# Keys, values and first queries of two cross-attention layers in one pipeline of token blocks

## The chip, the core and the metric

The kernel runs on one core of a Trainium2 chip. The metric is the device time of one execution in microseconds (us), and less is better. The core has a matrix engine (TensorE, PE in the rows; its weight loads are listed as PEld), a vector engine (VectorE, DVE), a scalar engine (ScalarE, ACT), GpSimd (POOL), and a queue that issues transfers (SyncE, SP). The engines run their own instruction streams and meet only at semaphores. TensorE runs at one of two clock levels, 1.2 and 2.4 GHz; the rows show the granted level as a fraction of the higher one (0.50 and 1.00).

## What is computed

Two cross-attention layers over 4096 query tokens (`x`) and 3202 context tokens (`ctx`), all 512 features wide:

```python
# layer 0: 8 heads of 16
Q0 = x @ W_q;  K0 = ctx @ W_k;  V0 = ctx @ W_v          # 512 -> 128 each
x1 = ffn(x + softmax(Q0 K0^T / 4) V0 @ W_o)
# layer 1: 16 heads of 32
kv = layernorm(ctx; mean, var) * gamma + beta
K1, V1 = split(kv @ Wkv.T)                               # 512 -> 512 each
Q1 = layernorm(x1) @ Wq.T
out = ffn(x1 + softmax(Q1 K1^T / sqrt(32)) V1 @ Wo + bo)
```

Only the products `Q0`, `K0`, `V0`, `K1`, `V1` and the norm of `ctx` are touched by the change. Everything after them is the same code in both kernels.

## The kernel before

All activations are kept feature-major: 512 features are four tiles of 128 partitions (`KT` = 4), and tokens run along the free axis in blocks of 512 (`NB`). Every float32 operand is split into a rounded part ("hi", float32r) made by ScalarE and a remainder ("lo") made by VectorE; each product is the three matmuls hi*hi, hi*lo, lo*hi. A product of 512 inputs is therefore 12 matmuls.

`build` (L1635) calls the phases one after the other. A phase (L43) ends by clearing its semaphores and a barrier of all engines. In order: `project("kv")` (L1653), `project("pq0")` (L1659), attention of layer 0 (`a0`), the middle (`m`: end of layer 0 and the queries of layer 1), attention of layer 1 (`a1`), the ending (`e`).

`project` (L115) does one input. First `split_weights` (L63) brings the weights through a two-deep stage, in pieces of one 128-row tile: SP loads, ScalarE copies to hi, VectorE subtracts to lo, and SP waits for that before it loads two pieces on. This block of code ends before the first token block is loaded. Then the token blocks run as a software pipeline: while the products of block n are made, the steps that prepare block n+1 are put in between by `interleave` (L208) at places given as fractions of the products. For the keys and values ("kv", 7 blocks, the last of 130 tokens) the steps of a block are: split x (L274, L327); mean by 8 matmuls with a matrix of 1/512 over both halves (L382); centre (L333); square and split the squares (L279, L281, L339); variance by 8 matmuls; square root (L286); reciprocal (L344); multiply by it (L345); gamma and beta (L348); split the normed block (L291, L354). Then 16 products of a block: 1 of K0, 4 of V0 (128 columns each), 4 of K1, 4 of V1 (the token tiles are the stationary side for the values), in a ring of 4 PSUM banks and 4 output buffers. The first product of a block waits for the last preparing step of it:

```python
if i == 0:
    pe.wait_ge(dve_steps, n * NDVE + NDVE)
pe.wait_ge(lo_done[s], before)
```

Keys are stored as [hi/lo, feature, token], values as [head, token in tile, tile, 16 or 32], so that a value store writes pieces of 64 or 128 bytes.

The queries ("pq0", 8 blocks) have one product a block, in one slot of the ring, so that ScalarE can only empty the next product when the 8 stores of the last one (64 KB each, one per head) have landed.

The middle phase (`m`, printed only in part here) already does a norm in another form for the queries of layer 1: `presum` (L1458, L1461) adds the four feature tiles on VectorE, one float32 matmul (L1583) gives the mean or variance, gamma is multiplied into the weights once (L1511), the product is made from the centred values, and its result is multiplied by 1/std (L1487) and gets the bias `beta @ W` (made once by single-column matmuls, L1605) on ScalarE and VectorE (L1384, L1491).

## Time and profile before

| | us |
|---|---|
| median of 3 runs (5737.87 to 5742.69) | 5738.86 |
| profiled execution, its own time | 5741.43 |
| its span | 5739.7 |
| weights of "kv" | 0 to 28.9 |
| "kv" until its first product | 28.9 to 68.3 |
| "kv" products | 68.3 to 306.6 |
| end of phase | 306.6 to 311.4 |
| "pq0" with its end | 311.4 to 392.1 |
| attention 0, middle, attention 1, ending | 392.1 to 5739.7 |

All times below are from the span's start of that execution. A busy time of TensorE counts overlapping records, so the distance between the starts of two matmuls says how fast they go, not the length of one record. "<-" names what an engine waited for.

### The profile page before, as it was taken

The page shows a single profiled execution, that of the slowest core. Times are in us where ns is not written, and L with a number is a line of the kernel's source. Part 1 is how long each engine was busy: PE and PEld are TensorE (multiplying, and loading weights), DVE is VectorE, ACT ScalarE, POOL GpSimd, SP SyncE. Part 2 cuts the span into 40 slices and gives each one's busy share as a digit, 9 for nine tenths or more (in the row PEclk, how much of TensorE's full clock was granted, in tenths as well). Part 3 has the DMA queues.
Part 4 walks back from the last instruction along what each step waited for, and adds up shares of the span by engine and source line. Part 5 has one row for each costly group of instructions (what it writes and reads, how often), then busy time and mean ns, then how long its engine had stood idle before and what let it go on. Part 6 is the DMA issues. An engine that isn't in the chain of part 4 may idle for free. (4 is left out here: it accounts for less than half of the span.)

```text
span 5739.7 us, 103849 instructions
## 1 busy us (share of the span) xinstructions
PE 5364.3 (93%) x28676; PEld 3368.1 (59%) x28676; DVE 3997.0 (70%) x6906; ACT 3200.2 (56%) x5849; POOL 2329.3 (41%) x1156
## 2 busy tenths in 40 slices
PE   5959999999979799999999999999999998899999
PEld 4834444444447565655565656555565664677777
DVE  4439888888847688888787878878788886332231
ACT  3317777777733256666666666666666665222222
POOL 0000000000000068888787888878788887000000
PEclk9969999999979899999999999999999999899999
DMA  3451111111144321111111111111111111322220
GB/s 99 125 132 30 37 37 37 37 36 37 28 140 120 108 66 41 39 41 28 40 39 42 39 29 39 41 39 40 28 39 41 41 28 44 111 96 81 81 88 22
DMA packets 328588, 325.61 MB, mean 57 GB/s; under 512 B 184624, under 2 KB 192688, under 8 KB 326064
## 3 DMA queue, kind: packets, MB, share of 16 engines
q1 hardware_dynamic: 328112, 319.92, 21.0%
q8 instruction: 218, 3.57, 0.3%
q14 instruction: 258, 2.11, 0.1%
HBM read 219.18 MB, written 100.53 MB: 56 GB/s over the span
## 5 line engine op out<-in xcount | busy, mean ns | idle before, releaser
L777 DVE TENSOR_REDUCE a_maxes<-a_mscore 128x1 f32<-128x458 f32 (+4 forms) x5376 | 3039.4, 625 | 668.7 <-PE a_mscore L836 640.3
L760 ACT ACTIVATE a_prob<-a_score 128x512 f32<-128x512 f32 x4992 | 2633.6, 598 | 1271.2 <-PE a_score L845 1260.6
L845 PE MATMUL a_score<-a_q,a_k 97*128 97x512 f32 (+1 forms) x4992 | 1993.4, 434 | 54.3 <-DMA a_q<-row 31.6
L836 PE MATMUL a_mscore<-a_k,a_qm 96*128 96x458 f32 (+4 forms) x5376 | 1901.1, 417 | 69.8 <-DMA a_k<-k 56.0
L864 PE MATMUL a_acc<-a_prob,a_v 128*32 128x512 f32 x9984 | 1613.0, 608 | 0.0
L836 PEld LDWEIGHTS a_mscore<-a_k,a_qm 96*128 96x128 f32 (+1 forms) x5376 | 1479.1, 310 | 192.1 <-issue 71.9
L726 POOL TENSOR_TENSOR a_added<-a_added,a_prob 128x1024 f32<-128x1024 f32 x640 | 1527.8, 2387 | 55.5 <-POOL a_added L726 0.2
L845 PEld LDWEIGHTS a_score<-a_q,a_k 97*128 97x128 f32 (+1 forms) x4992 | 924.8, 195 | 1028.1 <-ACT a_prob L760 534.9
L723 POOL TENSOR_TENSOR a_added<-a_prob 128x1024 f32<-128x1024 f32 x128 | 305.3, 2385 | 2053.7 <-ACT a_prob L760 2043.3
L859 PE MATMUL a_acc<-a_prob,a_ones 128*1 128x512 f32 x2048 | 965.1, 593 | 0.0
L864 PEld LDWEIGHTS a_acc<-a_prob,a_v 128*32 128x32 f32 x9984 | 293.4, 109 | 304.4 <-issue 155.7
L1136 DVE TENSOR_TENSOR e_hl<-e_h,e_hh 128x512 fp32r<-128x512 f32 x128 | 88.5, 692 | 457.4 <-ACT e_hh L1085 457.4
L1081 ACT ACTIVATE e_h<-e_hp,e_bias 128x512 f32<-128x512 f32 x128 | 88.2, 689 | 548.5 <-PE e_hp L1193 548.5
L739 POOL TENSOR_TENSOR a_total<-a_total,a_vsum 128x512 f32<-128x512 f32 x128 | 165.9, 1296 | 387.0 <-DVE a_vsum L791 386.9
L859 PEld LDWEIGHTS a_acc<-a_prob,a_ones 128*1 128x1 f32 x2048 | 129.0, 82 | 310.9 <-issue 310.9
L791 DVE TENSOR_REDUCE a_vsum<-a_prob 128x128 f32<-128x384 f32 x512 | 288.7, 585 | 22.3 <-ACT a_prob L760 22.3
L1193 PE MATMUL e_hp<-e_xh,w_hi 128*128 128x512 f32 x512 | 203.3, 397 | 4.1 <-DVE e_xl L1128 4.1
L1193 PE MATMUL e_hp<-e_xh,w_lo 128*128 128x512 f32 x512 | 203.1, 397 | 0.0
L1193 PE MATMUL e_hp<-e_xl,w_hi 128*128 128x512 f32 x512 | 203.0, 397 | 0.0
L736 POOL TENSOR_TENSOR a_total<-a_added 128x512 f32<-128x512 f32 x128 | 166.3, 1299 | 19.4 <-POOL a_added L730 18.1
L730 POOL TENSOR_TENSOR a_added<-a_added,a_prob 2x512 f32<-2x512 f32 x128 | 163.9, 1281 | 11.2 <-ACT a_prob L760 0.2
L746 ACT ACTIVATE a_acc_sb<-a_acc 97x512 f32<-97x512 f32 (+1 forms) x192 | 114.9, 598 | 72.2 <-PE a_acc L859 60.4
(188 smaller groups left out, 3905.9 us busy)
## 6 DMA issues: line engine op xcount, KB each, us to landing
a_qm<-q SPq DMA_DIRECT2D x384, 64.0 KB, 1.8
a_q<-q SPq DMA_DIRECT2D x384, 64.0 KB, 1.8
acc<-a_acc_sb SPq DMA_DIRECT2D x384, 64.0 KB
e_part<-acc SPq DMA_DIRECT2D x90, 256.0 KB, 3.4
a_k<-k SPq DMA_DIRECT2D x48, 416.0 KB, 5.8
q<-m_qout SPq DMA_DIRECT2D x128, 128.0 KB, 2.3
e_wo<-wo_split SPq DMA_DIRECT2D x32, 512.0 KB, 4.1
k<-kv_out SPq DMA_DIRECT2D x30, 512.0 KB, 2.7
```

What stands on the lines that cost most here:

```text
L723: pool.tensor_tensor(added[:], prob[:, 1:3], prob[:, 4:6], ALU.add).then_inc(add_done, 1)
L726: pool.tensor_tensor(added[:], added[:], prob[:, 3 * i + 1:3 * i + 3], ALU.add).then_inc(add_done, 1)
L736: pool.tensor_tensor(total[:], added[:, 0], added[:, 1], ALU.add).then_inc(add_done, 1)
L739: pool.tensor_tensor(total[:], total[:], vsum[:], ALU.add).then_inc(add_done, 1)
L760: act.activation(prob[:, t], score[SCORES[it.j][t]][:], ACT.Exp, scale=SCALE).then_inc(exp_done, 1)
L777: dve.tensor_reduce(maxes[j][:, t, c:c + 1], mscore[u % UNIT_BANKS][:, 0:wide], AX.X, ALU.max).then_inc(unit_read, 1)
L791: dve.tensor_reduce(vsum[:, cols], prob[:, ON_VECTOR[0]:ON_VECTOR[-1] + 1, cols].rearrange("p t c -> p c t"), AX.X, ALU.add).then_inc(vsum ...
L836: pe.matmul(mscore[u % UNIT_BANKS][:, 0:wide], qm[j][r:r + ROW, t:NB:NB // P], kt[kk][r:r + ROW, at:at + wide], start=True, stop=True).the ...
L845: pe.matmul(score[SCORES[it.j][t]][:], kt[it.k][r:r + C, i * P:(i + 1) * P], qt[it.j][r:r + C, :], start=True, stop=True).then_inc(score_d ...
L859: mm = pe.matmul(acc[c * 32:c * 32 + 1, :], ones[:], total[:] if what[0] == "sum" else prob[:, what[1]], start=(i == 0), stop=not after)
L864: mm = pe.matmul(acc[c * 32:c * 32 + 32, :], vt[kk][:, L.FIRST[half] + at, :], prob[:, what], start=(i == 0), stop=not after)
L1193: mm = pe.matmul(hp[m % 2][:], W1[a][:, k, m * P:(m + 1) * P], (xh, xl)[c][:, k], start=(t == 0), stop=(t == 3 * KT - 1))
```

## The change

`project` and `split_weights` go. One phase, `front`, does all of it, unrolled in full. Weights come as five whole transfers, between those of the tokens. The eight query blocks stand at the head; the first K0/V0 products, the weights' gains and the bias products lie between them. The norm takes the form that the middle has: VectorE adds feature tiles (`presum`), one float32 matmul gives the mean or variance, the products of K1 and V1 are made from the centred block, and the division comes behind them. For keys 1/std is a row vector (`rstd`, after `var`); for values it is a column per token tile (`rstdc`, after `varc`, four single-column matmuls). K0 and V0 of block n+2 are made in the middle of block n. The last block is 130 tokens wide, without padding; the pad columns are stored as zeros from an own transfer. Helpers that are cut only issue one instruction with its waits.

```diff
-    project(nc, "kv", ctx_t, S,
-            {"k0": a["L0_xattn_W_k"], "v0": a["L0_xattn_W_v"], "k1": a["L1_xattn_Wkv"][:, 0:D], "v1": a["L1_xattn_Wkv"][:, D:2 * D]},
...
-    project(nc, "pq0", x, T, {"q0": a["L0_xattn_W_q"]}, [("raw", "q0", "items", q[0])])
+    front(nc, "kv", ctx_t, x, a["L0_xattn_W_k"], a["L0_xattn_W_v"], a["L1_xattn_Wkv"], a["L1_xattn_ln_kv_g"],
+          a["L1_xattn_ln_kv_b"], a["L0_xattn_W_q"], k, v, q[0])
...
+        prod = [ps(f"prod{i}", [P, NB]) for i in range(5)]
+        mean, var, varc = ps("mean", [P, NB]), ps("var", [P, NB]), ps("varc", [P, KT])
...
+        @block.sync
...
+            load_weight("wq", small[0], w_q0)
+            load_xq(0)
+            load_xq(1)
+            load_weight("wk0", small[1], w_k0)
+            load_weight("wv0", small[2], w_v0)
+            load_ct(0)
...
+            load_weight("wk1", yc[:], w_kv1[:, 0:D])
+            load_xq(2)
+            load_weight("wv1", sq[:], w_kv1[:, D:2 * D])
+            load_xq(3)
+            load_ct(1)
...
+            for i in range(QBLOCKS):
+                if i + 4 < QBLOCKS:
+                    load_xq(i + 4)
+                store_q(i)
+                if i == 1:
+                    store_first(0)
+            load_ct(2)
+            store_first(1)
+            for n in range(BLOCKS):
+                for m in range(KT):
+                    store_keys(n, m)
+                if n + 3 < BLOCKS:
+                    load_ct(n + 3)
+                if n + 2 < BLOCKS:
+                    store_first(n + 2)
+                for m in range(VT[n]):
+                    store_values(n, m)
...
+        @block.scalar
...
+            halve_q(2)
+            split_xq(4)
+            act.wait_ge(bias_made, 2)
+            act.activation(biask[:], var[:, 0:KT], ACT.Copy).then_inc(bias_done, 1)
+            act.activation(biasv[:], mean[:], ACT.Copy).then_inc(bias_done, 1)
+            halve_q(3)
+            split_xq(5)
+            act.wait_ge(bias_done, 2)
+            square(0)
+            halve_q(4)
+            split_xq(6)
+            split_x(1)
+            halve_q(5)
+            split_xq(7)
+            deviation(0)
...
+        @block.vector
...
+            def presum(src, to, w, i, before, done):
+
+                dve.tensor_tensor(pair[:, :, 0:w], src[:, 0:2, 0:w], src[:, 2:4, 0:w], ALU.add).then_inc(pair_done, 1)
+                dve.wait_ge(pair_done, i + 1)
+                dve.wait_ge(*before)
+                dve.tensor_tensor(to[:, 0:w], pair[:, 0, 0:w], pair[:, 1, 0:w], ALU.add).then_inc(done, 1)
...
+            split_weight(4, WV1, gained[1])
+            sum_x(0)
+            halve_q(3)
+            split_xq(5)
+            centre(0)
+            halve_q(4)
+            split_xq(6)
+            sum_squares(0)
+            split_x(1)
+            halve_q(5)
+            split_xq(7)
+            invert(0)
+            halve_q(6)
+            split_yc(0)
+            halve_q(7)
+            halve_first(1)
+            for n in range(BLOCKS):
+                if n + 1 < BLOCKS:
+                    sum_x(n + 1)
+                if n + 2 < BLOCKS:
+                    split_x(n + 2)
+                scale_key(n, 0)
+                scale_key(n, 1)
+                if n + 1 < BLOCKS:
+                    centre(n + 1)
+                halve_key(n, 0)
+                halve_key(n, 1)
+                scale_key(n, 2)
+                if n + 1 < BLOCKS:
+                    sum_squares(n + 1)
+                scale_key(n, 3)
+                halve_key(n, 2)
+                if n + 1 < BLOCKS:
+                    split_yc(n + 1)
+                halve_key(n, 3)
+                if n + 2 < BLOCKS:
+                    halve_first(n + 2)
+                if n + 1 < BLOCKS:
+                    invert(n + 1)
+                for m in range(VT[n]):
+                    value(n, m)
...
+        @block.tensor
...
+            def find_variance(n):
+                pe.wait_ge(sqsum_done, n + 1)
...
+                for m in range(VT[n]):
+                    tokens = min(P, W[n] - m * P)
+                    pe.matmul(varc[0:tokens, m:m + 1], sqsum[:, m * P:m * P + tokens], inv_d[:, 0:1], start=True,
+                              stop=True)
+                pe.matmul(var[:, 0:W[n]], inv_d[:], sqsum[:, 0:W[n]], start=True, stop=True).then_inc(var_done, 1)
...
+            def key(n, m):
+                if m == 0:
+                    pe.wait_ge(ycl_done, n + 1)
+                    pe.wait_ge(w_lo, len(W_ORDER))
+
+                    if n + 1 < BLOCKS:
+                        pe.wait_ge(v0_done, n + 2)
...
+                elif n == 0:
+                    pe.wait_ge(ql_done, QBLOCKS)
+                else:
+                    pe.wait_ge(v1_done, (n - 1) * KT + m)
+                products(prod[m], WK1, slice(m * P, (m + 1) * P), (ych[n % 2], ycl[n % 2]), W[n]).then_inc(k1_made, 1)
...
+            queries(0)
+            queries(1)
+            first(0)
+            queries(2)
+            biases()
+            queries(3)
+            find_mean(0)
+            queries(4)
+            queries(5)
+            find_variance(0)
+            queries(6)
+            queries(7)
+            first(1)
+            for n in range(BLOCKS):
+                key(n, 0)
+                key(n, 1)
+                if n + 1 < BLOCKS:
+                    find_mean(n + 1)
+                key(n, 2)
+                key(n, 3)
+                if n + 2 < BLOCKS:
+                    first(n + 2)
+                if n + 1 < BLOCKS:
+                    find_variance(n + 1)
+                for m in range(VT[n]):
+                    value(n, m)
```

`biases` is 16 single-column float32 matmuls (`beta @ W` for keys, into `var`) and 4 of 512 columns (for values, into `mean`). `first(n)` is the 12 matmuls of K0 and the 48 narrow ones of V0. The value step `value(n, m)` on VectorE reads PSUM once: product times `rstdc` plus `biasv`.

## Rows read from the trace of the kernel before

**Rows 1.** The page's first part: busy time, share, instructions of each engine

```profile
PE 5364.3 (93%) x28676; PEld 3368.1 (59%) x28676; DVE 3997.0 (70%) x6906; ACT 3200.2 (56%) x5849; POOL 2329.3 (41%) x1156
```

**Rows 2.** Busy time of each engine by stage, up to the attention

```profile
core 0: us, PE busy (x) PEld busy (x) DVE busy (x) ACT busy (x) POOL busy (x), PEclk, DMA share, GB/s
0.00:28.90 28.90, 0.00 (x0) 0.00 (x0) 7.88 (x16) 8.79 (x17) 0.20 (x4) 1.00 0.29 91
28.90:68.30 39.40, 7.36 (x16) 4.96 (x16) 17.27 (x14) 11.41 (x7) 0.00 (x0) 0.88 0.24 80
68.30:306.60 238.30, 226.69 (x1140) 191.63 (x1140) 112.12 (x99) 82.12 (x116) 0.00 (x0) 0.96 0.48 121
306.60:311.40 4.80, 0.00 (x0) 0.00 (x0) 0.00 (x0) 0.58 (x1) 0.00 (x0) 0.98 0.47 74
311.40:392.10 80.70, 34.94 (x96) 25.18 (x96) 24.59 (x20) 21.21 (x20) 0.00 (x0) 0.69 0.61 160
```

**Rows 3.** Waits from 28.9 to 312: us in total, times, longest us

```profile
PE kv_prod L408 <- DVE kv_zl L354: 23.5, 6, 12.8
```

**Rows 4.** Waits from 312 to 392, the same columns

```profile
PEld pq_prod L408 <- DVE pq_xl L327: 39.2, 6, 21.2
ACT pq_out L302 <- DMA q<-pq_out: 17.6, 7, 7.5
```

**Rows 5.** VectorE in order of time, two blocks' centring: start, us, operation

```profile
114.08 2.29 DVE L333 TENSOR_TENSOR kv_xc<-kv_xt,kv_mean 128x2048 f32<-128x2048 f32 x1 [1.80 <-PE kv_mean L382]
...
151.77 2.29 DVE L333 TENSOR_TENSOR kv_xc<-kv_xt,kv_mean 128x2048 f32<-128x2048 f32 x1 [1.79 <-PE kv_mean L382]
```

**Rows 6.** TensorE in order of time, in "kv" and in the middle phase

```profile
90.27 0.39 PE L408 MATMUL kv_prod<-kv_zh,kv_k_hi 128*128 128x512 f32 x1
...
95.96 0.39 PE L408 MATMUL kv_prod<-kv_v_hi,kv_zl 128*128 128x512 f32 x1
...
111.30 0.28 PE L408 MATMUL kv_prod<-kv_v_hi,kv_xh 128*128 128x128 f32 x1
111.41 0.28 PE L408 MATMUL kv_prod<-kv_v_hi,kv_xl 128*128 128x128 f32 x1
...
1636.68 4.71 PE L1605 MATMUL m_var<-m_gb,m_sq 128*128 128x1 f32 x32
...
1756.17 1.02 PE L1583 MATMUL m_mean<-m_ysum,m_inv_d 128*128 128x512 f32 x2
1757.26 0.40 PE L1555 MATMUL m_prod<-m_xl,m_w_hi 128*128 128x512 f32 x1
```

**Rows 7.** Stretches: start of the products, around a block's start, a load of queries

```profile
68.30:72.30 4.00, 3.95 (x9) 3.17 (x10) 2.11 (x1) 0.00 (x0) 0.00 (x0) 0.50 0.00 0
...
104.00:106.00 2.00, 0.06 (x1) 0.00 (x0) 2.00 (x1) 1.82 (x2) 0.00 (x0) 1.00 0.92 145
106.00:108.00 2.00, 1.76 (x5) 1.39 (x6) 1.50 (x2) 0.57 (x1) 0.00 (x0) 0.60 0.92 144
...
321.00:323.00 2.00, 0.00 (x0) 0.00 (x0) 0.00 (x0) 0.00 (x0) 0.00 (x0) 0.50 1.05 402
```

**Rows 8.** Groups of VectorE: form, count, busy us and mean ns of one, idle before

```profile
L327 DVE TENSOR_TENSOR kv_xl<-kv_xt,kv_xh 128x2048 fp32r<-128x2048 f32 x6 | 13.7, 2292 | 9.7 <-ACT kv_xh L274 9.7
L363 DVE TENSOR_TENSOR kv_out<-kv_prod,kv_out 128x512 fp32r<-128x512 f32 x30 | 20.7, 689 | 62.2 <-ACT kv_out L302 62.2
L344 DVE RECIPROCAL kv_rstd<-kv_std 128x512 f32<-128x512 f32 x6 | 20.1, 3353 | 10.7 <-ACT kv_std L286 10.7
L1491 DVE SCALAR_TENSOR_TENSOR m_qout<-m_scaled,m_biasq,m_qout 128x512 fp32r<-128x512 f32 x32 | 23.8, 745 | 1.1
```

**Rows 9.** The middle phase, one block's stretch, columns as in rows 2

```profile
1757.00:1798.00 41.00, 38.76 (x162) 29.98 (x160) 30.18 (x35) 15.36 (x20) 0.00 (x0) 1.00 0.45 135
```

**Rows 10.** Transfers from 312 to 392: count, size, median us from issue to landing

```profile
pq_xt<-in_x SPq DMA_DIRECT2D x8, 1024.0 KB, 5.6
```

**Rows 11.** Start of the attention in order of time

```profile
392.15 1.28 ACT L760 ACT_TABLE_LOAD   x1 [6.91 <-PEq L60]
```

More of the change, by code:

```diff
@@ L905, in _ @@
                             weigh(it.n, it.k, b)
-def blocks_of(eng):
-    B = T // NB
-    with eng.Fori(0, B // 2 - 1) as i:
-        yield i * 2, 0, i, True, True
-        yield i * 2 + 1, 1, i, True, True
-    yield B - 2, 0, B // 2 - 1, True, False
-    yield B - 1, 1, B // 2 - 1, False, False
 TERMS = ((0, 0), (0, 1), (1, 0))
```

671 lines of the change are left out of this document (388 added, 283 removed).

## The prediction

> **What bounds the kernel now.** The page's first line comes first: TensorE is busy for 93% of the span [rows 1], so on the average it is the bound, but an average says nothing about the part that is changed. The second view is the busy time by stage [rows 2]. The change replaces what lies before 392.1; the rest of the span, 5739.7 - 392.1 = 5347.6, is the same code. In those 392.1 TensorE is idle for the 28.9 of the weights, nearly idle for the next 39.4 (7.4 busy), close to full in the 238.3 of the products, idle for 4.8 at the phase's end, and less than half busy in the 80.7 of the queries. So the first 68.3 are a start-up that nothing covers, the middle 238.3 are TensorE's, and the queries are bound by something else.
>
> The waits say by what. In the products of keys and values the one wait of TensorE that counts is for the last step of the norm, the low half of the normed block: 23.5 in six times, of which 12.8 once at the start, so about 2.1 a block later [rows 3]. In the queries the weight load waits for the split of x (39.2), and ScalarE waits for the eight stores of the last product before it may empty the next one (17.6) [rows 4]: a chain of load, split, product, store, with one slot.
>
> A period of "kv" is 151.77 - 114.08 = 37.7 [rows 5]. It can be counted. From 90.27 to 95.96 stand 25 steps of 512-column matmuls, 0.2275 each; a 128-column one follows the last at 0.11 [rows 6]. A block has 12 + 48 + 48 of the wide (24.6), 48 narrow (5.3), and 16 wide for mean and variance (3.7): 33.6. With the 2.1 of waiting that is 35.7. The missing 2.0 is clock: after the idle time at the block's start the granted clock reads 0.60 in a stretch of 2.0, where it was 1.00 before, and at the first product 9 matmuls took 4.0 at 0.50, which is 0.44 each [rows 7]. So 2.1 idle costs about 4 in all.
>
> **The change, part by part: the loop.** The new loop has per full block 24.6 of wide products and 5.3 of narrow ones as before. Mean and variance are now one float32 matmul each. The middle has them: two records from 1756.17, and the products behind go on at their own pace from 1757.26 [rows 6]; less one 0.23, that is 0.86 for the two records of one matmul, 1.7 for both in place of 3.7. New are the four single-column matmuls for `varc`; the middle's 32 records of this kind took 4.71, 0.147 each [rows 6], and four are eight records, 1.2. Sum 32.8.
>
> Does anything else need longer? VectorE, from the rows of its forms [rows 8], per block: three passes of 2048 (split x, centre, split the centred) 6.9; two partial sums, each half a 2048 pass and a 512 one, about 3.7; eight 512-wide passes on keys (4 x 0.69 + 4 x 0.745) 5.7; four for values at 0.745, 3.0; K0's remainder 0.7; reciprocal 3.4. Sum 23.4, 9 below TensorE. ScalarE was busy 82.1 of the 238.3 of the products [rows 2], 13 a block, and loses one pass of 2048: about 11. VectorE's order matters more than its sum: from the start of key(n, 0) the block's own chain is centre(n+1) once the mean is made at 6.4 (ends 8.9), square 10.9, sum of squares 12.9, split 16.6, while `find_variance` stands at 20 in TensorE's stream and key(n+1, 0), which needs the split, at 32.8. The reciprocal ends at about 26 and delays value(n, 0), made at 24; its bank is needed again at 35.5. So I find no wait in the steady state and cost the waits at 0.5 a block, with 0 and 4.8 (the old period back) as ends. The middle's steady stage is the nearest case: TensorE busy 38.8 of 41.0 at clock 1.00 [rows 9].
>
> The removed `rstd` product, gamma and beta passes and the split of the squares (two passes of 2048, four of 512, and one of 2048 on ScalarE) lay beside TensorE's work; their removal pays only by ending the 2.1 wait and the clock that it costs.
>
> Blocks 0 to 3: 4 x 32.8 = 131. Block 4 makes the short first(6), 28.9. Block 5 has no `first` and short statistics, 22.9. Block 6 has 48 matmuls of 130 columns and 24 of 512, 11. Waits 3. The loop is 197.
>
> **The head.** It is a chain over three engines. VectorE's work in it: 8 splits of query blocks 18.3, their 8 remainders 5.5, three small weights 2.1, eight gain products of 512 at 0.69 or less 5.5, two large weight remainders 4.6, two splits of context 4.6, betas 1.2, sum of x 1.9, centre 2.3, squares 1.9, reciprocal 3.4, split 2.3, two K0 remainders 1.4: 55. TensorE's at the high level: queries 21.8, two `first` 16.0, biases 4.7/2 x 2 = 4.7 (16 single-column matmuls are 32 records) plus 4 x 0.86, together 8.1, statistics 2.9: 49. Transfers: 8 MB of queries, 2 of context, 2.75 of weights in, about 5 out, at 402 GB/s [rows 7] 44; a single MB needs 5.6 [rows 10]. I therefore walk the order of the three streams. Estimated times from the span's start: first query block in at 6.5, split 10.7; products 0 and 1 done 18.2 (the first at 0.44 a matmul); context block 0 split 17.3, first(0) 18 to 26; query 2, 29; biases 29 to 37; query 3, 39.7. Meanwhile VectorE has made gains, splits and weight remainders without a gap and sums x by 38.9. Mean 40.6; but VectorE takes halve_q(3) and split_xq(5), both behind the bias copies on ScalarE, before centre(0), which ends at 47.9. Square 49.8; halve_q(4) and split_xq(6) come before the sum of squares, which ends at 56.5. TensorE has been idle since about 50. Then variance at the low level 3.5, query 6 and 7 7, first(1) 8, and ScalarE's copy of V0, for which key(0, 0) waits: 76. On VectorE's side the split of the centred block ends near 70. Block 2's context is queued behind all query stores (eight issues each) and lands at about 80; it is needed by TensorE at 88.
>
> So loop start 76, with 66 (VectorE's 55, a first load, and the last V0) and 108 (next part) as ends.
>
> **The end.** After the last product: one VectorE pass, a store of 256 KB, semaphores, barrier. "kv" has the same end today, 4.8 from the last TensorE work to the next phase [rows 2]. The barrier between the two phases and the second ramp fall away; they are inside the 392.1. The attention would start at 76 + 197 + 5 = 278 in place of 392.1 [rows 2, 11]: 114 less. Its own start (memsets, then loads) sees the same state, so nothing is given back later. The profiled execution would take 5741.4 - 114 = 5627. It lies 2.6 above the median of the runs, so the median comes to 5738.9 - 114 = 5625.
>
> Where the 114 comes from: the queries' stage 81 shrinks to what the head needs beyond today's start-up (76 - 68 = 8), 73; the products 238 to 197, 41.
>
> **A rule against it.** Seven blocks now cycle TensorE through eight banks, with a semaphore at every group of 12 matmuls. The rows show that a 2.1 gap was followed by a clock of 0.60 [rows 7], and that the middle, built alike, keeps 1.00 with 2.2 idle in 41.0, spread over several groups [rows 9]. The Trainium skill, "TensorE: Matmul & The Clock Gate", section "A second HAM failure mode: psum-queue depth-cycling", says that small idle times between groups as banks are cycled can make the clock swing between its two levels. By the page the loop could run long stretches at 1.2 GHz; by the middle's row it does not, and I side with the row and keep the other as a rival.
>
> **The rivals.**
> 1. *The head is TensorE's at the low level.* The queries' stage today reads a clock of 0.69 [rows 2], because its bursts are short. If the head's gaps do the same throughout, its 49 become 97 behind the first split at 10.7: loop start 108, time 5625 + 32 = 5657. For it: VectorE's 55 leaves gaps between products. Against it: first(0), biases and query 3 stand in one row, 21 of work without a wait.
> 2. *The loop keeps the old period.* A wait takes the removed one's place: SP stores keys, block load, K0/V0 and values in strict order, and the value stores in small pieces run at 145 GB/s with the transfer engines 0.92 busy [rows 7]. Six periods of 37.6: +29, 5654. Against it: 4.75 MB a block, of which 1.25 are slow, need 8.6 + 3.5/0.402 = 17 of 33.
> 3. *The clock falls in the loop* (the rule above): each wait between groups throws TensorE back to 0.44 a matmul. The whole loop would take nearly 197 more; the kernel becomes slower once more than 114 of the loop's 197 at the high level, 58%, run at the low one. Nine tenths of it: 5625 + 177 = 5802, slower than before.
> 4. *The change doesn't do what it says*: the head's three streams block each other so often that the queries still take their 81 beside the start-up of 68, and the loop keeps its period: 149 + 226 + 5 = 380, or 5739 - 12 = 5727.
>
> **How the numbers follow.** Forecast 0.70 (5625; its own ends are 5612, with head 66 and no waits, and 5645, with head 90 and waits of 1.5 a block). Rival 1 0.12, rival 2 0.13, rival 3 0.03, rival 4 0.02. The range 5605 to 5662 takes in the forecast and rivals 1 and 2, with 5 to 7 at either end for what the walk through the head may miss. A measurement of this kernel can tell about 0.2%, 11, from no change. Faster by more than that: 0.95; same 0.02; slower 0.03.
>
> **What would show it.** In the trace of the changed kernel: the first attention row near 278; VectorE's centring at a period of 32.8 to 33.5; TensorE's clock 1.00 from the first key product on; granted clock in the head between 0.6 and 0.9; the mean matmul at 0.86 and a `varc` record at 0.15; in the head, centre(0) about 7 after the mean is made, and TensorE idle before the variance of block 0; no wait of TensorE for VectorE over 1 in the loop. Wrong would be: waits for stores in the loop, a period over 35, key(0, 0) later than 90, or an attention, middle or ending that differs from 5347.6 by more than 5.

## The result, and the profile after

The changed kernel takes 5599.95 us, the median of 4 runs (5594.11 to 5608.29), against 5738.98 for the kernel before (5737.87 to 5742.69): a ratio of 0.9758, 95% interval 0.9741 to 0.9775. That is 139 faster where 114 were forecast, and 5 below the low end of the range. The profiled execution took 5599.11, with a span of 5597.3.

The page's first line of the changed kernel, which answers to [rows 1]:

```profile
PE 5326.1 (95%) x28684; PEld 3349.3 (60%) x28684; DVE 4013.6 (72%) x6947; ACT 3170.5 (57%) x5792; POOL 2330.6 (42%) x1156
```

Busy time by stage of the new phase, columns as in [rows 2]: the head until its chain breaks, the wait for the norm of block 0, the last of the head, the loop, the end:

```profile
0.00:57.00 57.00, 38.12 (x174) 29.56 (x174) 37.25 (x39) 30.27 (x27) 0.20 (x4) 0.93 0.96 303
57.00:67.00 10.00, 8.32 (x23) 6.28 (x24) 9.92 (x7) 3.65 (x4) 0.00 (x0) 0.54 0.40 70
67.00:78.57 11.57, 10.79 (x74) 9.71 (x72) 6.10 (x6) 4.20 (x5) 0.00 (x0) 1.00 0.65 109
78.57:268.70 190.13, 190.13 (x986) 159.13 (x987) 123.74 (x137) 56.77 (x68) 0.00 (x0) 1.00 0.61 147
268.70:275.90 7.20, 1.64 (x8) 0.41 (x5) 0.74 (x1) 0.00 (x0) 0.00 (x0) 0.90 0.48 73
```

In the loop TensorE is busy for all of its 190.13 at a granted clock of 1.00, where the products of before had 226.69 of 238.30 at 0.96 [rows 2]. All waits of TensorE from 0 to 270 (us in total, times, longest) stand in the head:

```profile
PE kv_prod L1043 <- DVE kv_ycl L866: 11.7, 1, 11.7
PE kv_varc L1110 <- DVE kv_sqsum L895: 7.3, 1, 7.3
PE kv_mean L1101 <- DVE kv_xsum L895: 1.5, 1, 1.5
PE kv_prod L1043 <- ACT kv_v0out L767: 0.8, 1, 0.8
```

The first is the start (no query block is split before 11.7), the second the wait ahead of the variance of block 0. The third and fourth are small. The granted clock of the head falls twice. The second fall stands behind the 7.3. The first comes with TensorE busy without a gap since 11.7, about 2 into the 32 single-column records of the key bias:

```profile
29.96 4.89 PE L1087 MATMUL kv_var<-kv_gb,kv_yc 128*128 128x1 f32 x32
```

```profile
30.00:32.00 2.00, 2.00 (x21) 2.00 (x19) 2.00 (x2) 0.28 (x1) 0.00 (x0) 1.00 1.00 330
32.00:34.00 2.00, 2.00 (x12) 2.00 (x11) 0.63 (x1) 0.00 (x0) 0.00 (x0) 0.52 1.07 368
34.00:36.00 2.00, 2.00 (x6) 1.48 (x7) 0.00 (x0) 0.10 (x1) 0.00 (x0) 0.50 0.97 287
```

The 0.93 of the first stage is even somewhat too high: the clock reads 1.00 there from 0 on, but the first products, from 11.67, go at 0.43 a matmul, which is the pace of the low level. The three engines in order of time (start, us, operation): the first key product; a mean, the second matmul of the product around it and VectorE's centring in two blocks; the single-column matmuls with the variance behind them; ScalarE's copy of V0 in two blocks; and the attention's first row:

```profile
78.57 0.47 PE L1043 MATMUL kv_prod<-kv_ych,kv_wk_hi 128*128 128x512 f32 x1 [0.78 <-ACT kv_v0out L767]
...
116.63 1.02 PE L1101 MATMUL kv_mean<-kv_xsum,kv_inv_d 128*128 128x512 f32 x2
...
117.69 2.29 DVE L917 TENSOR_TENSOR kv_yc<-kv_ct,kv_mean 128x2048 f32<-128x2048 f32 x1 [0.17 <-PE kv_mean L1101]
...
117.72 0.39 PE L1043 MATMUL kv_prod<-kv_ycl,kv_wk_hi 128*128 128x512 f32 x1
...
131.00 1.00 PE L1110 MATMUL kv_varc<-kv_inv_d,kv_sqsum 128*128 128x1 f32 x8
...
131.20 0.60 ACT L767 ACTIVATE kv_v0out<-kv_prod 128x512 f32<-128x512 f32 x1 [4.71 <-PE kv_prod L1050]
...
131.86 1.10 PE L1112 MATMUL kv_var<-kv_sqsum,kv_inv_d 128*128 128x512 f32 x2
...
150.21 2.29 DVE L917 TENSOR_TENSOR kv_yc<-kv_ct,kv_mean 128x2048 f32<-128x2048 f32 x1 [0.17 <-PE kv_mean L1101]
...
163.72 0.60 ACT L767 ACTIVATE kv_v0out<-kv_prod 128x512 f32<-128x512 f32 x1 [4.71 <-PE kv_prod L1050]
...
275.93 1.28 ACT L411 ACT_TABLE_LOAD   x1 [10.37 <-PEq L60]
```

A period is 163.72 - 131.20 = 32.52, and so is the centring's, 150.21 - 117.69, against 37.7 in [rows 5]. The attention starts at 275.93 in place of 392.15 [rows 11]: 116.2 earlier. That is what the changed code brings, and 142.4 (5739.7 - 5597.3) is what the span lost. The other 26 lie in stages whose code is the same. Each stage is read from one profiled execution of each kernel. Here are those stages of the kernel before: attention 0 from its first row to its last row maximum, its end (to the middle's first product), the middle, attention 1, the ending:

```profile
392.15:1560.25 1168.10, 1119.54 (x6660) 554.12 (x6660) 1029.97 (x1870) 887.10 (x1688) 0.00 (x0) 0.96 0.18 37
1560.25:1632.30 72.05, 34.40 (x127) 8.79 (x124) 13.12 (x16) 25.25 (x45) 0.00 (x0) 0.55 0.38 113
1632.30:1988.95 356.65, 322.45 (x1312) 248.11 (x1312) 245.24 (x265) 127.24 (x164) 0.00 (x0) 0.96 0.40 119
1988.95:4920.61 2931.66, 2819.50 (x15921) 1692.08 (x15921) 2316.63 (x4265) 1828.16 (x3468) 2329.14 (x1152) 0.98 0.16 41
4920.61:5739.66 819.05, 799.45 (x3408) 643.23 (x3408) 230.23 (x344) 208.29 (x327) 0.00 (x0) 0.99 0.23 76
```

And the same stages of the changed kernel:

```profile
275.93:1439.60 1163.67, 1115.95 (x6659) 553.17 (x6660) 1030.15 (x1869) 887.28 (x1688) 0.00 (x0) 0.96 0.18 37
1439.60:1500.60 61.00, 23.39 (x127) 6.75 (x125) 13.19 (x17) 24.64 (x45) 0.00 (x0) 0.74 0.43 134
1500.60:1859.14 358.54, 324.15 (x1312) 249.06 (x1312) 245.21 (x265) 127.69 (x164) 0.00 (x0) 0.96 0.40 119
1859.14:4781.65 2922.51, 2815.03 (x15921) 1691.38 (x15921) 2317.17 (x4265) 1828.27 (x3467) 2330.37 (x1152) 0.98 0.16 41
4781.65:5597.33 815.68, 798.54 (x3408) 643.79 (x3408) 230.10 (x344) 207.73 (x327) 0.00 (x0) 0.99 0.24 77
```

The counts are the same, the times are not: -4.4, -11.1, +1.9, -9.2, -3.4, together -26.1. Two of them have a place that can be seen.

**The end of attention 0**: 72.05 with a clock of 0.55, or 61.00 with 0.74. Low time, worked out as length x (1 - clock) x 2, is 65 against 32. It begins at the last row maximum. The first 24.0 behind it, before and after:

```profile
1560.21:1584.21 24.00, 22.74 (x91) 6.15 (x90) 3.61 (x3) 15.77 (x30) 0.00 (x0) 0.65 0.03 7
...
1439.66:1463.66 24.00, 22.35 (x125) 6.62 (x125) 3.61 (x3) 20.76 (x40) 0.00 (x0) 1.00 0.03 7
```

After, ScalarE has made its 40 exponentials by then; before, TensorE fell to its low level on the way, and only 30 of them are done.

**Attention 1**: it works through 128 items, each one head and one block of 512 queries; they are counted here from one row maximum to the next. In five of them (33, 49, 65, 81 and 97) the loop over pairs of heads jumps back. These five together take 144.4 before and 127.2 after, 17.2 less, while the rest of the stage is 8.1 longer after. Item 81 takes 29.61 against 25.04. These are the waits inside it; "issue" is time in which the engine waited for nothing that the profile shows. Before:

```profile
ACT a_prob L760 <- PE a_score L845: 14.8, 9, 3.8
...
PE a_mscore L836 <- issue: 2.6, 1, 2.6
...
PE a_score L845 <- issue: 2.0, 1, 2.0
```

After:

```profile
ACT a_prob L411 <- PE a_score L496: 10.1, 9, 3.6
...
PE a_score L496 <- issue: 2.0, 1, 2.0
```

The stop of 2.6 in front of a `mscore` is gone, and the granted clock over the item is 0.93 in place of 0.88. It is so in all five: before, TensorE stops 2.2 to 2.6 in front of a `mscore`, 12.5 together, and after it never does. The low time of the five is 34 before and 17 after.

### The profile page after: what moved, and what is told of

The parts are those of the page before. It is cut to its first block and busy times, and to the rows that moved or that the text cites. A ratio compares the mean times of both kernels' runs of the same rounds, so it can differ in the third digit from the quotient of the medians.

```text
span 5597.3 us, 103454 instructions
## 1 busy us (share of the span) xinstructions
PE 5326.1 (95%) x28684; PEld 3349.3 (60%) x28684; DVE 4013.6 (72%) x6947; ACT 3170.5 (57%) x5792; POOL 2330.6 (42%) x1156
## 5 line engine op out<-in xcount | busy, mean ns | idle before, releaser
L387 POOL TENSOR_TENSOR a_total<-a_added 128x512 f32<-128x512 f32 x128 | 165.9, 1296 | 21.1 <-POOL a_added L381 19.8
L397 ACT ACTIVATE a_acc_sb<-a_acc 97x512 f32<-97x512 f32 (+1 forms) x192 | 114.8, 598 | 65.1 <-PE a_acc L510 57.0
```

The lines of the kernel that those rows point to most:

```text
L387: pool.tensor_tensor(total[:], added[:, 0], added[:, 1], ALU.add).then_inc(add_done, 1)
```

## The experiments

Two questions: is the gain of the front what it was forecast to be, for the reasons given; and what moves 26 us in code that nobody touched? For the second there were three candidates: the time since the start (or the transfers that are still under way), the phase of the clock, and the place of the code. In what follows "front" is the time to the attention's first row, "end" the end of attention 0 with its low time in brackets, "five" the sum of the five items, each from one profiled execution. The two references: before 392.1, 72.1 (65), 144.4; after 275.9, 60.9 (32), 127.2.

### A pause at the start of attention 0

VectorE writes an unused tile 8 times (e1) or 210 times (e2) ahead of its fills; e3 is the changed kernel once more, and e4 is the kernel before with the pause of e1.

```diff
+        PAUSE = 8 if name == "a0" else 0
...
+            for i in range(PAUSE):
+                dve.wait_ge(paused, i)
+                dve.memset(pad[:], 0.0).then_inc(paused, 1)
             for ap, value in FILLS:
                 dve.memset(ap, value).then_inc(filled, 1)
```

> The changed kernel with about 5 us of vector memsets (8 of 512 columns) ahead of attention 0's own; nothing else is changed. In the profiles of before and after, attention 0 (its activation table load to the middle's first product) took 1240.2 and 1224.7 with the same instructions; of the 15.5, 11 lie behind the last row maximum, where the granted clock is 0.50 for the last items of before and 1.00 for those of after. Theory P (the clock's falls land by the moment at which the attention starts and ends): attention 0 takes some value between 1224 and 1241 that need not be the changed kernel's; the total is 5 longer than the changed kernel's, plus or minus 15. Theory S (the new front leaves something that makes the attention faster: buffers, code, transfers): attention 0 stays at 1224.7 within 2, total 5 longer.

> The changed kernel with about 116 us of vector memsets (210) ahead of attention 0's, so that the attention starts near the 392 of the kernel before. Theory P: attention 0 takes a value between 1224 and 1241; if the moment counted from the kernel's start decides, it is before's 1240 and the total is that of the kernel before less 0 to 10. Theory S: attention 0 at 1224.7 within 2, total 116 above the changed kernel, 23 under the kernel before.

> The changed kernel as it is, to see how much one kernel's stages move from run to run. Theory P: with the moments unchanged up to the jitter of the transfers, attention 0 and 1 may each move by up to 10; total 5594 to 5610. Theory S: 1224.7 and 2922.5 again within 2.

> The kernel before with the same 5 us pause ahead of attention 0. Theory P: attention 0 between 1224 and 1241, total 5744 plus 5, less up to 25: it can get faster through a pause. Theory S: 1240.2 within 2, total 5744.

| | median (lowest to highest) | ratio, 95% | front | end | five |
|---|---|---|---|---|---|
| e1 | 5606.25 (5595.27 to 5615.08) | 0.9746, 0.9728 to 0.9764 | 275.5 | 72.0 (65) | 122.4 |
| e2 | 5736.65 (5728.3 to 5753.05) | 0.9981, 0.9969 to 0.9993 | 276.0 | 72.3 (65) | 125.2 |
| e3 | 5599.64 (5595.45 to 5606.44) | 0.9743, 0.9725 to 0.976 | 274.8 | 61.4 (34) | 128.5 |
| e4 | 5747.7 (5740.65 to 5760.72) | 1.0001, 0.9991 to 1.001 | 390.4 | 62.1 (35) | 145.9 |

The first 24.0 behind the last row maximum in e1, and in e4:

```profile
1444.32:1468.32 24.00, 22.74 (x91) 6.14 (x90) 3.61 (x3) 15.77 (x30) 0.00 (x0) 0.65 0.03 7
...
1563.45:1587.45 24.00, 22.35 (x125) 6.62 (x125) 3.61 (x3) 20.76 (x40) 0.00 (x0) 1.00 0.03 7
```

In these profiles about 5 us of pause (5.1 by the rate of e2) turn the end of the changed kernel into that of the kernel before, to the last exponential, and the other way round in e4. So the end has two values and belongs to neither kernel.

The medians do not carry these 11. e1 is 6.6 above e3 and e4 is 3.0 above the 5744.75 of the kernel before in the same comparison, so less the pause of 5.1 they differ by +1.5 and -2.1, not by +11 and -10. The profiled executions of e1 and e2 are the slowest and the second slowest of theirs. The executions of one kernel lie up to 25 apart, and the slower ones show a lower mean clock (e1: 0.975 at 5595.27, 0.970 at 5615.08). The likely reading is that the end takes either value from one execution to the next; it isn't shown, as only one execution of each has a profile.

The pause of e2 was longer than meant:

```profile
L450 DVE MEMSET a_pad<- 128x512 f32 x210 | 101.8, 485 | 41.2 <-DVE a_pad L450 36.2 <-PEq L60 5.0
```

101.8 + 36.2 = 138.0. With that taken off, its median is 5598.7, that of the changed kernel: time since the start explains none of the 26. The five items take 122 and 125 in e1 and e2, 128.5 in e3, and 146 in e4. Whatever makes them long goes with the program of the kernel before, not with a moment that is 5 later. And the stop in front of `mscore` is there in all five items of e4 (2.4 to 2.6), and in none of e1, e2 and e3.

### TensorE's gaps at the end of attention 0 filled

In the last item of attention 0 a further matmul of 256 columns follows each score product (26 in all; the result is not read), in the kernel before (e5) and in e1 (e6).

```diff
                     scores(it, t)
+                    if it.last and name == "a0":
+                        if t == 0:
+                            pe.wait_ge(unit_read, H * QB * UNITS)
+                        for u in range(1):
+                            pe.matmul(mscore[u % UNIT_BANKS][:, 0:256], qm[it.j][0:ROW, 0:P], kt[it.k][0:ROW, 0:256],
+                                      start=True, stop=True)
                     due(it, t)
```

> The kernel before, with one matmul of 256 columns more behind each of the 26 score products of attention 0's last item; nobody reads their results. They are pure extra work for TensorE, about 0.12 each at the high level, 3 in all. Theory P (in the last item ScalarE is the bound and TensorE has gaps; whether its clock falls there, to 0.50, is decided by the moment, and at 0.50 TensorE becomes the bound): filled gaps keep the level at 1.00, the time from the last row maximum to the middle's first product goes from 72.1 to 60 to 64, in spite of the extra work. Rival (the low clock goes with the end, but doesn't set its length; the stage is longer for another reason, such as the stores): 72 to 75, and the whole no faster.

> The changed kernel with the 5 us pause, whose end of attention 0 took 72.0 with 65 of low clock, and the same 26 extra matmuls. Theory P: 60 to 64, and the whole about 10 faster than with the pause alone. Rival: 72 to 75.

| | median | ratio, 95% | front | end | five |
|---|---|---|---|---|---|
| e5 | 5722.46 | 0.9964, 0.9951 to 0.9976 | 391.1 | 65.7 (41) | 123.7 |
| e6 | 5607.32 | 0.9764, 0.9745 to 0.9783 | 276.8 | 65.1 (40) | 123.0 |

The first 24.0 of the end in e5:

```profile
1563.54:1587.54 24.00, 22.50 (x126) 8.76 (x124) 3.60 (x3) 17.89 (x35) 0.00 (x0) 0.86 0.03 7
```

The clock falls later (0.86 over the 24.0), and the end lands between its two values: 24 and 25 less low time, 6.4 and 6.9 less end. Expected was a clock that stays up, and an end of 60 to 64. Both kernels come out alike, so the low time is tied to the end's length, but the fill has not removed it. For e6 the whole was also expected about 10 faster than e1, and it is not (5607.32 against 5606.25). The fill also brought a surprise: the five items of the kernel before fell from 144 to 124, though nothing in attention 1 was edited. What it changed for that stage is where TensorE's later instructions lie, and the whole became 19.8 faster.

### TensorE's program moved by a few instructions

20, 7 or 30 unused single-column matmuls ahead of the first work of TensorE. Each is two records, and they go at 0.213 a record, the pace of the low level: 20 take 8.7, 7 take 3.2 and 30 take 13.0. In the kernel before, TensorE has no other work until 39.6, so 7 and 20 end in its idle time, while 30 put off its first statistic from 39.61 to 42.63. Their result is not read. Kernel before (e7: 20, e13: 7, e14: 30):

```diff
             if ln is not None:
                 pe.wait_ge(consts_done, 3)
+                for _ in range(20):
+                    pe.matmul(prod[0][:, 0:1], inv_d[:], inv_d[:, 0:1], start=True, stop=True)
```

Changed kernel (e8: 20, e15: 30):

```diff
+            pe.wait_ge(consts_done, 2)
+            for _ in range(20):
+                pe.matmul(varc[:, 0:1], inv_d[:], inv_d[:, 0:1], start=True, stop=True)
             queries(0)
```

> The kernel before with 20 single-column matmuls ahead of its first statistic, while TensorE waits for the first block; they only shift the place of all later TensorE instructions in its program. In attention 1 the five items at which the loop over pairs of heads jumps back (33, 49, 65, 81, 97) took 144.4 in the kernel before and 145.8 with the pause, against 127.2, 122.5 and 128.6 in the three profiles of the changed one. Theory L (where the code lies decides how long the engines wait for instructions after the jump): this sum moves by more than 5, either way, the rest stays. Rival (it is set by what ran before, or by chance): 144 to 146 again.

> The changed kernel with the same 20 matmuls at its start. Theory L: the sum over the five items leaves 122 to 129 by more than 5, either way, if the shift crosses a boundary; it can also stay. Rival: 122 to 129. The front itself: its start waits for the first queries anyway, so attention 0 starts at 275 to 277 as before, unless TensorE's level at the first product differs.

> The kernel before with 7 single-column matmuls ahead of its first statistic, in TensorE's idle time. With 20 of them the five items with a jump in attention 1 took 127.3 in place of 144.4, and the median fell by 31. Theory L (place of the code): the sum over the five items is near 144 or near 125, by where the shift of 7 puts the loop; all else of attention 1 within 8. Rival (20 extra matmuls changed something else, such as the moment): a value between, 130 to 140.

> The same with 30. Theory L: near 144 or near 125 again. Rival: between. If both shifts give 125, the kernel before stood at an unlucky place, and the median is near 5712 to 5725; where the end of attention 0 also stays at the high clock it is 5712, otherwise 5723.

> The changed kernel with 30 of them at its start. Theory L: its place is a good one, a shift can at best leave it: five items 119 to 129, or near 144, with a median of 5600 or 5617. Attention 0 starts at 275 to 278 either way.

| | median | ratio, 95% | front | end | five |
|---|---|---|---|---|---|
| e7, before, 20 | 5711.54 | 0.9948, 0.9933 to 0.9963 | 392.9 | 61.1 (32) | 127.3 |
| e13, before, 7 | 5719.06 | 0.9957, 0.9943 to 0.9972 | 394.5 | 61.1 (34) | 132.8 |
| e14, before, 30 | 5717.48 | 0.9955, 0.994 to 0.997 | 395.1 | 72.8 (66) | 129.8 |
| e8, after, 20 | 5599.22 | 0.975, 0.9733 to 0.9766 | 275.8 | 61.5 (32) | 123.4 |
| e15, after, 30 | 5609.37 | 0.9765, 0.9748 to 0.9781 | 278.1 | 73.0 (66) | 128.8 |

Item 81 in e7, waits as above:

```profile
ACT a_prob L762 <- PE a_score L847: 10.7, 9, 4.2
...
PE a_score L847 <- issue: 2.4, 1, 2.4
```

It reads like the changed kernel's item: the 2.6 ahead of `mscore` is gone. Each of the three shifts makes the kernel before 24 to 31 us faster by the medians, although the front gets 0.8 to 2.9 longer by work that is of no use; the shifts of 20 and 30 do not make the changed kernel faster. A later moment alone did not do this in e4. So the kernel before stood at a bad place, and leaving it is worth about the 25 that the forecast missed. In which stages the 24 to 31 lie can't be read from one profile each: the profiled executions lie 8 (e7), 8 (e13) and 18 (e14) above their medians, and e14's, the slowest of five, has the long end.

The expectation for e13 set 144 or 125 for the place of the code against 130 to 140 for something else, and 132.8 lies in the second range. The traces settle it. The stop in front of `mscore` stands in all five items of before and e4 and in no item of the five in the 15 other profiles, e13 among them. What is left is clock. The low time of the five is 34 in both profiles with the stop, and 0 (e12) to 27 (e13) in the others, whose sums are 119.1 plus half of it, to within 1.5 (e10: 3.1). For before that line gives 136; the 8 above it, of 17.2 between the two references, is what can be put down to the stops, and the other half is low clock. The rest of attention 1, expected to stay, is 5 to 8 longer in e7, e13 and e14 than the 2787 of before, and 9 longer in e4.

Held against the shifted kernels, the change is worth what was forecast: the three ratios of before average 0.9953, those of e3, e8, e15 and the changed kernel 0.9754, and (0.9953 - 0.9754) x 5739 = 114. The interval of each ratio is about 9 us to either side, so that it is 114 to the us is luck.

### The terms of the front

**e9: VectorE's passes put back.** Two unused passes of 2048 (2.28 each) in each of the first five blocks of the loop, one before `sum_squares`, one behind `split_yc`.

```diff
+            def again(i):
+                dve.wait_ge(junk_done, i)
+                dve.wait_ge(yc_done, i // 2 + 2)
+                dve.tensor_tensor(junk[:], yc[:], yc[:], ALU.subtract).then_inc(junk_done, 1)
...
+                if n + 1 < B:
+                    again(2 * n)
                 if n + 1 < BLOCKS:
                     sum_squares(n + 1)
...
                     split_yc(n + 1)
+                if n + 1 < B:
+                    again(2 * n + 1)
```

> The changed kernel with two more VectorE passes of 2048 elements in each of the loop's first five blocks (23 us in all), one ahead of the sum of squares and one behind the split of the centred block: where the old form of the norm had the split of the squares and the multiplication by 1/std. Their results are not used. Theory T (the loop is TensorE's, VectorE has 9 a block to spare, and the removed passes were worth nothing by their own length): attention 0 starts at 275 to 278, as in the changed kernel. Rival V (the shorter chain on VectorE is what pays): 2.3 to 4.6 a block, attention 0 at 287 to 299.

Median 5604.9, ratio 0.9753 (0.9736 to 0.9769); front 276.7, 0.8 later. That VectorE loses work is worth nothing by itself. Of the 5.2 that a period lost (37.7 to 32.5), 1.1 is TensorE's own work for the statistics (3.7 to 1.7 + 0.86), and the other 4 are the wait and its clock, counted at about 4 from the rows of before. That these went because no step of VectorE stands last before a product is argued from the order of the streams, and no run has put them back.

**e12: the statistics twice.** Mean and variance matmuls of blocks 1 to 6 issued twice, TensorE's work alone being longer.

```diff
+                if n > 0:
+                    pe.matmul(mean[:, 0:W[n]], inv_d[:], xsum[:, 0:W[n]], start=True, stop=True)
                 pe.matmul(mean[:, 0:W[n]], inv_d[:], xsum[:, 0:W[n]], start=True, stop=True).then_inc(mean_done, 1)
...
+                if n > 0:
+                    pe.matmul(var[:, 0:W[n]], inv_d[:], sqsum[:, 0:W[n]], start=True, stop=True)
                 pe.matmul(var[:, 0:W[n]], inv_d[:], sqsum[:, 0:W[n]], start=True, stop=True).then_inc(var_done, 1)
```

> The changed kernel with the float32 matmul of the mean and that of the variance issued twice in every block but the first: 10 of 512 columns and 2 of 130 more. Theory T (the loop is TensorE's, each record on its path): 10 x 0.86 + 2 x 0.3 = 9 later, attention 0 at 284 to 286. Rival (the loop is bound by VectorE, ScalarE or stores, and TensorE waits anyway): 0 to 3.

Median 5611.39, ratio 0.9767 (0.975 to 0.9784); front 286.7, 10.8 later. Each us of TensorE counts in full, and TensorE waits for nothing in the loop: the loop is bound by it. Of the 1.8 above the 9, most is one fall of the clock behind the single-column matmuls (0.70 and 0.50 in the two stretches of 2 from 134), which e11 shows more plainly.

**e10: the queries in their own phase again**, behind the new pipeline, by the old `project`.

```diff
-            queries(0)
-            queries(1)
             first(0)
-            queries(2)
             biases()
...
+    project(nc, "pq0", x, T, {"q0": a["L0_xattn_W_q"]}, [("raw", "q0", "items", q[0])])
```

> One half of the change alone: the new pipeline for keys and values, but without queries in its head; they are made behind it by the old phase. Theory (the walk through the head): without the queries' 24 on VectorE and 22 on TensorE the first key product comes at about 45 in place of 78.6; loop 192 and end 5 give 242, and the old query phase 81: attention 0 at 323, so 69 of the 116 come from the keys' and values' pipeline and 47 from the queries' place. Rival (the head is set by the weights' and the norm's chain, the queries only fill its gaps): first key product at 65 or later, attention 0 at 343 or more, and the queries' place is worth 67 or more.

Median 5664.77, ratio 0.9858 (0.9837 to 0.9878). The variance of block 0, the first key product, and SP's first transfer for the queries:

```profile
43.74 1.87 PE L1415 MATMUL kv_varc<-kv_inv_d,kv_sqsum 128*128 128x1 f32 x8 [6.36 <-DVE kv_sqsum L1216]
...
57.91 0.47 PE L1348 MATMUL kv_prod<-kv_ych,kv_wk_hi 128*128 128x512 f32 x1 [0.78 <-ACT kv_v0out L1106]
...
255.29 0.83 SPq L589 DMA_DIRECT2D pq_stage<-in_L_xattn_W_q  x2
```

The front is 335.4. So the 116.2 split in two: 392.1 - 335.4 = 56.7 for the new form of keys and values, and 335.4 - 275.9 = 59.5 for the queries' place (they take 80.1 apart, and 78.57 - 57.91 = 20.7 in the head). Expected were 69 and 47, and by the rival 67 or more for the queries; neither came. The first key product was expected at 45 and came at 57.91. From the start of the mean to that of the variance the norm's chain (mean, centre, square, sum) takes 43.74 - 36.29 = 7.5 here, and TensorE waits for 6.4 of it, having no query to make. In the changed kernel the same stretch is 58.68 - 44.74 = 13.9, as VectorE has two splits and a remainder of queries within it.

**e11: the centring of block 0 earlier.** In VectorE's order `centre(0)` and `sum_squares(0)` each go ahead of a query's remainder and split.

```diff
             sum_x(0)
+            centre(0)
             halve_q(3)
             split_xq(5)
-            centre(0)
+            sum_squares(0)
             halve_q(4)
             split_xq(6)
-            sum_squares(0)
```

> The changed kernel with another order on VectorE in the head: centre(0) straight behind sum_x(0), and the sum of squares ahead of halve_q(4) and split_xq(6). Theory (the 7.3 that TensorE idles before the variance of block 0, and the low clock behind it, come from VectorE's order): the variance starts at 53 in place of 58.7, the first key product and attention 0 come 4 to 6 earlier, at 270 to 272. Rival (something else is as late, such as ScalarE's square behind its query work): 0 to 2.

Median 5601.16, ratio 0.9743 (0.9726 to 0.9759): no gain. The wait before the variance is gone, but TensorE waits 2.4 and 5.0 for splits of queries and 3.0 for the mean's sum instead (1.5 after), and the first key product comes at 78.08, only 0.5 earlier. From mean to variance it is now 54.62 - 45.46 = 9.2. So VectorE's order does make that wait, as the theory had it, but the time is not to be had: the wait moves. In the profiled execution, the slowest of the four (5611.17 against 5597.78 for the fastest), the attention even started 6.2 later, at 282.1, and the cause is not in the head. Four stretches of its loop, the single-column matmuls standing from 97.99 to 98.85:

```profile
97.00:99.00 2.00, 2.00 (x20) 2.00 (x20) 1.15 (x2) 0.60 (x1) 0.00 (x0) 1.00 0.28 103
99.00:101.00 2.00, 2.00 (x4) 0.88 (x5) 0.00 (x0) 0.23 (x2) 0.00 (x0) 0.51 1.03 251
101.00:103.00 2.00, 2.00 (x7) 1.64 (x6) 1.53 (x2) 0.61 (x2) 0.00 (x0) 0.64 0.98 266
103.00:105.00 2.00, 2.00 (x10) 1.61 (x9) 2.00 (x2) 0.03 (x1) 0.00 (x0) 1.00 0.93 335
```

The granted clock falls for about 3.5 right behind them, with TensorE busy without a gap, and again at 133, 167 and 201, behind the same matmuls of the next three blocks. Four times 3.5 at half speed cost 7. The changed kernel's TensorE has the same instructions in the same order in its loop and keeps 1.00 in its profile. What decides between the two isn't known.

## Why the prediction was right in the front and wrong in the sum

**The head: right within 3.** First key product at 78.57, forecast 76. The idle time stands where the walk through the three streams put it: TensorE waits 7.3 before the variance of block 0 (6.5 forecast), which starts at 58.68 (56.5). Part of this is luck: the mean came 4.1 late (44.74 for 40.6), and the centring made up for half of it, as only one step of a query was left before it. The clock was low for the first products, for 6.8 from 32.1, and for 10.2 around that wait; the second of the three, behind the biases' single-column records, was not in the walk. Rival 1, the low level throughout, would have given 108. The cause of the wait was named rightly: without the queries on VectorE the chain takes 7.5 (e10), with three steps of them within it 13.9, and with another order the wait is gone (e11). But it is not time lost to that order, since e11 gains only 0.5.

**The loop: right.** Forecast 32.8 and 0.5 of waiting a block, measured 32.5 and none. The mean matmul took 0.86 (116.63 to 117.72, the second matmul of the product behind it, less one 0.23 for the first), as counted from [rows 6]. The eight `varc` records took 0.86 (131.00 to 131.86), 0.108 each, where 0.147 from [rows 6] was used: a term 0.3 too large. That row was a mean over both levels of the clock. In the kernel before, the level falls within those 32 records, without a wait of TensorE, and the records stand 0.112 apart before 1639 and 0.213 behind it:

```profile
1636.68:1638.68 2.00, 2.00 (x20) 2.00 (x18) 1.76 (x3) 1.94 (x4) 0.00 (x0) 1.00 0.54 136
1638.68:1641.39 2.71, 2.71 (x15) 2.62 (x14) 2.25 (x2) 0.42 (x1) 0.00 (x0) 0.56 0.41 81
```

Rival 2 (the old period) is refuted by the period, and by e9, where 4.6 more of VectorE per block changes nothing.

**The clock rule: small, and real in a form that was not foreseen.** The Trainium skill, "TensorE: Matmul & The Clock Gate", section "A second HAM failure mode: psum-queue depth-cycling", speaks of small idle times between groups. In the loop there is no idle time, the clock is 1.00 throughout in the changed kernel, and rival 3 did not come; so no run here tests the page's case. What does come is a fall at the single-column matmuls without any idle time: in the loop four times in e11 and once in e12, at about 1.75 each, and in the head of the changed kernel once, for 6.8.

**The end: right.** The last product starts at 269.95, one step of 0.23 later the loop is over, and the attention starts 5.7 behind that, for 5. The sum of the front is 78.6 + 191.6 + 5.7 = 275.9 where 76 + 197 + 5 = 278 was forecast; of the 5 that the loop is shorter, 3 are the waits that did not come.

**The failed step** is "its own start sees the same state, so nothing is given back later", with the sentence before it that the rest of the span, 5347.6, is the same code. Same code was taken for same time. The rest took 5321.4. What the runs show in its place is that the time of this code depends on where TensorE's program lies: with nothing but 7, 20 or 30 unused matmuls ahead of it, the kernel before is 24 to 31 faster by the medians, and it is not faster with a pause that moves the moment alone (e4). In the two profiled executions the 26.1 lie as follows. 11.1 are the end of attention 0, which has two values: e1 and e4 show that each kernel's program can have either, and the medians don't bear them out as a lasting difference between the kernels. 17.2 are the five items in attention 1, of which 8.1 come back elsewhere in that stage. That the stop in front of `mscore` goes with the place of TensorE's code is shown by e5, e7, e13 and e14, where nothing of that stage was changed, and by both profiles that have the program of the kernel before unmoved (144 and 146, with the stop) against all the 15 others (119 to 133, without it); the low clock in these items makes up the other half. The last 5.9 (-4.4, +1.9, -3.4) have no cause that was found. The prediction had named a difference of over 5 there as a sign of being wrong, but gave the range no room for it: the terms outside the change carried no bounds at all. With 26 as their size, its low end would have been 5612 - 26 = 5586.

**Still open.** Which address or boundary matters for the stop; 7, 20 and 30 matmuls all leave the bad place. What sets how often the clock falls in the five items (low time 0 to 27 without the stop). How the 24 to 31 of the medians divide over the stages. Why the stage from the attention's first row to its last row maximum varies between 1162 and 1173 from kernel to kernel (pauses taken off). And that the end of attention 0 is chosen by the clock's phase is argued from the low time (32 to 35, or 65 to 66, with nothing between unless the gaps are filled); what sets the phase, and whether it changes from one execution to the next, was not measured.

No version beat the changed kernel: e3 and e8, at 5599.6 and 5599.2, are the same within their intervals.

## What to carry to other kernels

Where a norm stands before a product on the bound engine, move its division behind the product and add the feature tiles on the idle engine first: the gain can be counted as matmul steps at the rows' own spacing, to within 3 in 116 here. A small phase bound by a chain of load, split, product and store is worth more inside the start-up of a large one (20.7 in place of 80.1). And give the untouched rest of a long kernel bounds of its own: here it moved by 26 between two profiles, and 7 to 30 unused matmuls ahead of it moved the whole by 24 to 31, so a change of this size is only judged against a kernel before that has been shifted too.

## What the hardware showed that was not expected

- Code that is the same, instruction for instruction, takes 61 or 72 at the end of a phase, by whether TensorE falls to its low level in the last item (low time 32 or 65). In one profile each, a pause of 5 turned it both ways; in the medians it left no such difference.
- Unused matmuls at the start of the program, 7, 20 or 30 of them, made the kernel before 24 to 31 faster. A stop of 2.2 to 2.6 in each of five items at a loop's jump, for which the profile names no cause, went away with them.
- A gapless stream of matmuls can lose its clock at single-column records: within 32 of them in the head of the changed kernel (from 32.1, for 6.8) and in the middle of the kernel before (at 1639), and behind eight of them (0.86) in e11, for about 3.5, but not behind the same eight in the changed kernel.
- A single-column float32 record takes 0.108 to 0.112 at the high level and 0.213 at the low one. The 0.147 of the row of before was the mean of a group in which the level fell [rows 6].
- The granted clock reads 1.00 from the start of the changed kernel's profile, while its first products go at the low level's pace (0.43 each from 11.67), and so does it over the 8.7 of unused matmuls in e7 (0.213 each). At the start of a profile the spacing of the matmuls says more than the clock.
